# A vision tower on one core: group 0's patch embedding moved whole ahead of the class token's projections, the class chain on DVE behind the first normalisation

## The chip, the cores and the metric

The kernel runs on one core of one Trainium2 chip. The metric is the device time of one execution in microseconds (us). The engines are TensorE (PE, with its weight loads, PEld), VectorE (DVE), ScalarE (ACT), GpSimd (POOL) and SyncE (SP), which issues most of the transfers. Each engine runs its own instructions in order, and they wait for one another through semaphores.

## The reference

```python
patches = X.reshape(64, 3, 8, 28, 8, 28).transpose(0, 2, 4, 1, 3, 5).reshape(64, 64, 2352)
tokens = einsum('bpi,hi->bph', patches, W) + b              # 2352 -> 128
h = concatenate([class_token, tokens], axis=1) * pos_embed  # 65 rows per image
x = layernorm(h)
q, k, v = relu(x @ Wq.T + bq), relu(x @ Wk.T + bk), x @ Wv.T + bv   # 8 heads of 16
attn = softmax(einsum('bhnd,bhmd->bhnm', q, k) / (k.sum(-1, keepdims=True) + 1e-6))
h = h + (attn @ v) @ Wo.T + bo
# then layernorm twice, a shared swiglu network, and 2 of 8 experts by gates:
h = h + ffn(layernorm(h))
```

All is float32. The class token's row is the same in every image until attention has been done, so its normalised row, its q, k and v are computed once.

## The kernel before

The 64 images are worked in 8 groups of 8 images, 512 patch tokens each. The patch embedding of a group is a sum of 18 steps of 128 inputs (`NMAIN` = 18) and a tail of 48, in one PSUM bank `acc`; a step is two passes of PE in the profile. `patch(g, j0, j1)` issues the steps j0 to j1-1, and step 18 is the tail. The weights `w_patch` and the pixels `x_main` come in six pieces of three steps each (`PIECES`), each with its own semaphore. ACT's queue issues the loads of pieces 0 and 1 of the weights, then `const`, pieces 2 and 3, then the loads for the class token (`row_loads`: `rows`, `w_attn`, `bq_row`), and last pieces 4 and 5. SP's queue issues the pixels of group 0, then of group 1 as soon as the steps of group 0 have used a piece, then the weights of the feed-forward network.

Each engine has a prologue and then a `body(g)` for each group. `body(0)` is written out apart, so conditions on `last` (false for g = 0 alone) select what only group 0 has.

PE's prologue before (L638 to L657): 12 patch steps of group 0; wait for the class loads (`w_row`) and for the class row `hn_cls`; its transpose; 2 patch steps; wait for ACT's copy `hn_cls_t`; the class token's four small projections (q, k, v, and the bias bv through Wo) into bank `O`; 3 steps; transposes of `k_cls` and `qn_cls` into `C0`; the last step and the tail; `to_natural(0)` (transposes of `h_t` into `C1`); `AHEAD` = 6 steps of group 1; `normed_t(0)` (transposes of the normalised tokens `hn_nat`). Ahead of the bodies PE waits for `cdve` 19, that is for DVE's `k_sel`, which `k_sums` uses.

PE's body starts with `k_proj`, `q_proj`, `k_sums`, `v_proj`, `q_transpose`, then `score(g, 0)` to `score(g, 3)` with the steps of the next group between them (`fill`).

ACT's prologue before (L898 to L910): copy of `hn_cls_t`; copies of the two columns `k_cls_t` and `qn_cls_t`; four small copies of the class key into `k_bd`; `natural(0)` (`h_nat`); `normed_t(0)` (`hn_t`). Its body starts with a table load, `k_plain` (`k_t`), `k_blocks` (four copies into `k_bd`), `v_blocks` (two into `v_bd`), `q_masked` (two into `q_mask`). All ACT copies are recorded at the line of the helper `go`, L796.

DVE's prologue before (L1244 to L1297): the class row (`h_cls`, its moments, `hn_cls`); the class chain of 19 small operations that starts with `q_cls_raw` from bank `O` (wait for `cpe` 2) and ends with `k_sel` (L1292, which waits for `cact` 3, the two column copies of ACT) and `cc_col`; then `tokens(0)` (L1028, `h_t`), `norm1(0)` and `norm1_scale(0)` (`hn_nat`). Its body starts with `q_add` and `q_norm`, then the row maxima of the scores. POOL waits for `cdve` 16 ahead of its bodies, since `bias_residual` reads `bo2`.

Of the kernel before, what the change touches and what calls it, by code (L numbers as in the profile page):

```python
# [32 lines left out]
NPATCH = GRID * GRID  # L33
SEQ = NPATCH + 1
D = 128
IN_D = CHANNELS * PATCH * PATCH
NMAIN = IN_D // 128
# [13 lines left out]
AHEAD = 6  # L51
# [44 lines left out]
def vit_tower(nc, A, out):  # L96
    ctx = ExitStack()
    with ctx:
# [235 lines left out]
        def is_int(g, value):  # L334
            return isinstance(g, int) and g == value
# [55 lines left out]
        def _(pe):  # L391
# [7 lines left out]
            def patch(g, j0, j1):  # L399

                if j0 == 0:
                    need(pe, hT_done, g - 1)
                for j in range(j0, j1):
                    for i, (a, _) in enumerate(PIECES):
                        if j == a:
                            need(pe, x_in[i], g)
                            if isinstance(g, int) and g == 0:
                                pe.wait_ge(w_piece[i].sem, 16)
                    if j < NMAIN:
                        last = mm(acc[:, :], w_patch[:, j, :], x_main[:, j, :], start=(j == 0), stop=False)  # L410
                        if any(j == b - 1 for _, b in PIECES):
                            last.then_inc(x_used.sem, 1)
                    else:
                        need(pe, x_in[-1], g)
                        mm(acc[:, :], w_patch_tail[:, :], x_tail[:, :], start=False, stop=True)\  # L415
                            .then_inc(acc_full.sem, 1)
# [186 lines left out]
                last.then_inc(e_full.sem, 1)  # L603


            def class_scores():
                need(pe, cscore_done, GROUPS - 1)
                need(pe, hT_done, GROUPS - 1)
                for half in range(2):
                    last = nc.tensor.transpose(acc[:, half * 128:(half + 1) * 128],  # L610
                                               cls_scores[:, half * 128:(half + 1) * 128], ident)
                last.then_inc(tpe.sem, 1)
# [20 lines left out]
            def class_out():  # L633
# [1 line left out]
                mm(acc[0:IMAGES, 128:256], tc_attn_t[:, :], wo[:, :], start=True, stop=True).then_inc(tpe.sem, 1)  # L635


            patch(0, 0, 12)  # L638
            pe.wait_ge(w_first.sem, FIRST)
            pe.wait_ge(w_row.sem, ROW)  # L640
            pe.wait_ge(hcls_step.sem, 4)
            nc.tensor.transpose(B1[:, 0:128], hn_cls[:, :], ident).then_inc(cpe.sem, 1)
            patch(0, 12, 14)
            pe.wait_ge(cact.sem, 1)
            mm(O[:, 0:128], hn_cls_t[:, :], wq[:, :], start=True, stop=True)
            mm(O[:, 128:256], hn_cls_t[:, :], wk[:, :], start=True, stop=True)
            mm(O[:, 256:384], hn_cls_t[:, :], wv[:, :], start=True, stop=True)
            mm(O[:, 384:512], bv_col[:, 0:1].to_broadcast([128, 128]), wo[:, :], start=True, stop=True)\
                .then_inc(cpe.sem, 1)
            patch(0, 14, 17)  # L650
            pe.wait_ge(cdve.sem, 9)
            nc.tensor.transpose(C0[:, 0:128], k_cls[:, :], ident)
            nc.tensor.transpose(C0[:, 128:256], qn_cls[:, :], ident).then_inc(cpe.sem, 1)
            patch(0, 17, NMAIN + 1)
            to_natural(0)
            patch(1, 0, AHEAD)
            normed_t(0)  # L657

            def body(g, par):
                nxt, last = has_next(g), has_last(g)  # L660

                ahead = 0 if last else AHEAD

                def fill(j0, j1):
                    if nxt and j1 > ahead:
                        patch(g + 1, max(j0, ahead), j1)

                k_proj(g)
                if last and not is_int(g, 1):
                    gates(g - 1, TILES, 128)  # L670
                q_proj(g)
                if is_int(g, 1):
                    z_transpose(0)
                k_sums(g)
                v_proj(g)
                if is_int(g, 1):
                    gates(0, TILES, 128)
                    pe.wait_ge(wlo_done.sem, 4)
                if last:
                    ffn_in(g - 1, 0, TOK)  # L680
                    ffn_in(g - 1, 1, TOK)
                if not nxt:
                    class_scores()
                q_transpose(g)
                if last:
                    ffn_in(g - 1, 2, TOK)
                    ffn_in(g - 1, 3, TOK)
                fill(0, 1)
                score(g, 0)
                fill(1, 3)  # L690
                score(g, 1)
                fill(3, 5)
                prob_transpose(g, 0)
                fill(5, 6)
                prob_v(g, 0)
                score(g, 2)
                fill(6, 9)
                prob_transpose(g, 1)
                fill(9, 10)
                if not nxt:  # L700
                    expert(g - 1, 0, 128)
                prob_v(g, 1)
                if not nxt:
                    class_probs()
                score(g, 3)
                fill(10, 13)
                if not nxt:
                    counts(g - 1, TILES, 128)
                prob_transpose(g, 2)
                if nxt and last:  # L710
                    counts(g - 1, TILES, 128)
                fill(13, 14)
                if not nxt:
                    shared_out(g - 1, 0, 128, False)
                    shared_out(g - 1, 1, 128, False)
                    shared_out(g - 1, 2, 128, False)
                prob_v(g, 2)
                fill(14, 18)
                prob_transpose(g, 3)
                fill(18, NMAIN + 1)  # L720
                if nxt and last:
                    shared_out(g - 1, 0, 128, False)
                    shared_out(g - 1, 1, 128, False)
                elif not nxt:
                    shared_out(g - 1, 3, 128, True)
                    expert(g - 1, 1, 128)
                prob_v(g, 3)
                if nxt:
                    to_natural(g + 1)
                if nxt and last:  # L730
                    shared_out(g - 1, 2, 128, False)
                    shared_out(g - 1, 3, 128, True)
                    expert(g - 1, 0, 128)
                elif not nxt:
                    expert(g - 1, 2, 128)
                attn_transpose(g)
                if nxt and last:
                    expert(g - 1, 1, 128)
                out_proj(g)
                if nxt and last:  # L740
                    expert(g - 1, 2, 128)
                if nxt:
                    normed_t(g + 1)
                else:
                    class_values()
                if last:
                    expert(g - 1, 3, 128)
                if last:
                    expert(g - 1, 4, 128)
                if not nxt:  # L750
                    class_out()
                if nxt and last:
                    expert(g - 1, 5, 128)
                if last:
                    z_transpose(g)
                if not nxt:
                    expert(g - 1, 5, 128)
                if last:
                    expert(g - 1, 6, 128)
                    expert(g - 1, 7, 128)  # L760

            pe.wait_ge(cdve.sem, 19)
            groups(pe, body)

            L = GROUPS - 1
# [28 lines left out]
        def _(act):  # L794
# [102 lines left out]
                        act.dma_start(dst, src).then_inc(w_row.sem, 16)  # L897
            act.wait_ge(cpe.sem, 1)  # L898
            go(hn_cls_t[:, :], B1[:, 0:128]).then_inc(cact.sem, 1)
            act.wait_ge(cpe.sem, 3)  # L900
            go(k_cls_t[:, :], C0[:, 0:1]).then_inc(cact.sem, 1)
            go(qn_cls_t[:, :], C0[:, 128:129]).then_inc(cact.sem, 1)
            act.wait_ge(pool_init.sem, POOL_INIT)
            act.wait_ge(cact.sem, 3)
            for hp in range(HP):
                r = slice(32 * hp, 32 * hp + 32)
                go(k_bd[r, :, hp, NPATCH:SEQ], k_cls_t[r, 0:1].unsqueeze(2).to_broadcast([32, GROUP_IMAGES, 1]))\
                    .then_inc(cact.sem, 1)
            natural(0, 0)
            normed_t(0)  # L910

            def body(g, par):
                nxt, last = has_next(g), has_last(g)
                load_table(g, 0, ACT.Silu if last else ACT.Relu)
                k_plain(g)
                k_blocks(g)
                if is_int(g, 1):
                    z_out(0, TOK)
                v_blocks(g)
# [72 lines left out]
        def _(dve):  # L992
# [244 lines left out]
            def output(g, tiles, rows):  # L1237
# [16 lines left out]
            dve.wait_ge(hcls_step.sem, 3)  # L1254
            v.tensor_scalar(hn_cls[:, :], h_cls[:, :], cls_mv[:, 0:1], cls_rstd[:, 0:1], ALU.subtract, ALU.mult)\
                .then_inc(hcls_step.sem, 1)
            dve.wait_ge(cpe.sem, 2)
            v.tensor_tensor(q_cls_raw[:, :], O[:, 0:128], bq_row[:, :], ALU.add).then_inc(cdve.sem, 1)
            v.tensor_tensor(k_cls_raw[:, :], O[:, 128:256], bk_row[:, :], ALU.add).then_inc(cdve.sem, 1)
# [32 lines left out]
            v.tensor_scalar(k_sel[:, HEADS:16], const[:, C_HEAD:C_HEAD + HEADS], qn_cls_t[:, 0:1], None, ALU.mult)\  # L1292
                .then_inc(cdve.sem, 1)
            v.tensor_reduce(cc_col[:, :], cc_pick[:, :], AX.X, ALU.add).then_inc(cdve.sem, 1)
            tokens(0)
            norm1(0, 0)
            norm1_scale(0, 0)  # L1297


            def class_max():  # L1300
# [322 lines left out]
```

## Time and profile before

| | |
|---|---|
| median of three runs | 560.98 us (559.74 to 562.35) |
| span of the profiled execution | 562.2 us |
| PE busy | 502.9 us (89%) |
| DVE busy | 335.3 us (60%) |
| ACT busy | 179.7 us (32%) |
| POOL busy | 183.0 us (33%) |
| mean granted clock of PE | 0.923 |

The page gives no time of its own for the profiled execution beside its span, which is the time from the first to the last instruction. The busy shares are means over a start of about 100 us, in which the engines wait for one another, and a steady part up to about 460 us, in which PE is busy nearly all the time. The change is in the start, so its rows are read there.

### The profile page before, as it was taken

The page shows a single profiled execution, that of the slowest core. Times are in us where ns is not written, and L with a number is a line of the kernel's source. Part 1 is how long each engine was busy: PE and PEld are TensorE (multiplying, and loading weights), DVE is VectorE, ACT ScalarE, POOL GpSimd, SP SyncE. Part 2 cuts the span into 40 slices and gives each one's busy share as a digit, 9 for nine tenths or more (in the row PEclk, how much of TensorE's full clock was granted, in tenths as well). Part 3 has the DMA queues.
Part 4 walks back from the last instruction along what each step waited for, and adds up shares of the span by engine and source line. Part 5 has one row for each costly group of instructions (what it writes and reads, how often), then busy time and mean ns, then how long its engine had stood idle before and what let it go on. Part 6 is the DMA issues. An engine that isn't in the chain of part 4 may idle for free.

```text
span 562.2 us, 7098 instructions
## 1 busy us (share of the span) xinstructions
PE 502.9 (89%) x2241; PEld 353.4 (63%) x2241; DVE 335.3 (60%) x867; ACT 179.7 (32%) x334; POOL 183.0 (33%) x214
## 2 busy tenths in 40 slices
PE   5596885999999999999999999999999968698775
PEld 2244543855875587558755876587658756596563
DVE  0042358274776477647764777577756768935672
ACT  0015215342174216421642164216421652002320
POOL 6000006221271128112811182118211825226235
PEclk9788696599999999999999999999999998758988
DMA  8954150036004510451045104510000000000000
GB/s 342 366 179 175 45 187 1 0 112 211 22 0 131 193 41 1 132 179 53 0 131 174 57 0 129 172 61 1 20 1 0 2 19 1 0 1 1 18 2 21
DMA packets 14413, 44.71 MB, mean 80 GB/s; under 512 B 1721, under 2 KB 7090, under 8 KB 14386
## 3 DMA queue, kind: packets, MB, share of 16 engines
q1 hardware_dynamic: 12882, 42.39, 22.6%
q10 hardware_dynamic: 1504, 1.99, 1.1%
q8 instruction: 14, 0.23, 0.2%
q14 instruction: 13, 0.11, 0.1%
HBM read 42.24 MB, written 2.13 MB: 79 GB/s over the span
## 4 chain that ended last, share of the span: by engine, by line
PE 65%; DVE 17%; issue 7%; DMA 4%; POOL 4%; ACT 1%; ACTq 1%; DVEq 0%; POOLq 0%; SPq 0%
PE acc L410 21%; PE scores L471 6%; PE O L497 5%; PE B L396 4%; DMA bq_row<-in_bq_row 3%; DVE z_nat L1021 3%; PE acc L629 2%; DVE stats L1004 2%; PE B L453 2%; PE acc L415 2%; PE C L547 1%; POOL rstd L1446 1%; PE C L574 1%; DVE attn_nat L1113 1%; PE scores L549 1%
## 5 line engine op out<-in xcount | busy, mean ns | idle before, releaser
L410 PE MATMUL acc<-x_main,w_patch 128*128 128x512 f32 x288 | 141.4, 619 | 5.9 <-DMA w_patch<-in_w_patch 5.9
L410 PEld LDWEIGHTS acc<-x_main,w_patch 128*128 128x128 f32 x288 | 54.7, 200 | 50.3 <-issue 42.0
L1509 POOL TENSOR_TENSOR prod<-prod 128x512 f32<-128x512 f32 (+1 forms) x33 | 42.6, 1291 | 33.3 <-DVE prod L1233 33.3
L796 ACT ACTIVATE probs<-shift 128x512 f32<-128x512 f32 x32 | 20.4, 638 | 83.5 <-DVE shift L1073 83.5
L1502 POOL TENSOR_TENSOR hidden_lo<-silu,hidden_hi 128x512 fp32r<-128x512 f32 (+1 forms) x18 | 20.9, 1163 | 76.8 <-ACT hidden_hi L796 76.7
L497 PEld LDWEIGHTS O<-v_bd,probs_t 128*128 128x128 f32 x256 | 32.4, 195 | 21.2 <-ACT probs_t L796 11.9
L471 PE MATMUL scores<-k_bd,q_mask 128*128 128x260 f32 x128 | 38.9, 430 | 6.3 <-DVE shift L1073 3.1
L1069 DVE TENSOR_REDUCE row_max<-scores 128x8 f32<-128x520 f32 x32 | 22.3, 698 | 30.7 <-PE scores L471 30.3
L497 PE MATMUL O<-v_bd,probs_t 128*128 128x64 f32 (+1 forms) x256 | 35.4, 283 | 5.6 <-ACT probs_t L796 5.6
L1461 POOL TENSOR_TENSOR p_cls<-exp_cls,row_rec 128x16 f32<-128x16 f32 x16 | 5.4, 337 | 104.5 <-DVE row_rec L1088 100.0
L1442 POOL TENSOR_TENSOR rstd<-var,neg_half 128x4 f32<-128x4 f32 x8 | 8.1, 1015 | 87.0 <-DVE var L1017 87.0
L471 PEld LDWEIGHTS scores<-k_bd,q_mask 128*128 128x128 f32 x128 | 23.6, 205 | 19.0 <-DVE shift L1073 7.9
L796 ACT ACTIVATE probs_t<-B 128x512 f32<-128x512 f32 x32 | 19.0, 593 | 50.8 <-PE B L396 50.8
L1099 DVE TENSOR_TENSOR attn_patch<-O,row_rec 64x256 f32<-64x256 f32 x32 | 13.5, 422 | 32.4 <-PE O L497 31.9
L1021 DVE TENSOR_SCALAR z_nat<-h,mv,rstd 128x128 f32<-128x128 f32 (+1 forms) x33 | 28.8, 929 | 5.5 <-POOL rstd L1446 5.5
L1233 DVE TENSOR_TENSOR prod<-scores,comb 128x512 f32<-128x512 f32 (+1 forms) x33 | 22.6, 683 | 15.1 <-POOL routed L1516 9.8
L1233 DVE TENSOR_TENSOR prod<-C,comb 128x512 f32<-128x512 f32 (+1 forms) x33 | 22.0, 680 | 14.3 <-PE C L602 14.3
L600 PE MATMUL C<-w_eout_hi,hidden_hi 128*128 128x512 f32 (+1 forms) x66 | 29.2, 442 | 0.0
L600 PE MATMUL scores<-w_eout_hi,hidden_hi 128*128 128x512 f32 (+1 forms) x66 | 28.7, 435 | 0.0
L601 PE MATMUL C<-w_eout_lo,hidden_hi 128*128 128x512 f32 (+1 forms) x66 | 27.4, 415 | 0.0
L602 PE MATMUL C<-w_eout_hi,hidden_lo 128*128 128x512 f32 (+1 forms) x66 | 27.3, 413 | 0.0
L1511 POOL TENSOR_TENSOR prod<-prod 128x256 f32<-128x256 f32 (+1 forms) x33 | 26.2, 794 | 2.6
(239 smaller groups left out, 1052.6 us busy)
## 6 DMA issues: line engine op xcount, KB each, us to landing
x_main<-in_x_main SPq DMA_DIRECT2D x48, 768.0 KB, 4.2
out_tokens<-y_out SPq DMA_DIRECT2D x16, 128.0 KB, 2.5
w_patch<-in_w_patch ACTq DMA_DIRECT2D x6, 192.0 KB, 12.0
prod<-in_w_eout SPq DMA_DIRECT2D x2, 512.0 KB
x_tail<-in_x_tail SPq DMA_DIRECT2D x8, 96.0 KB, 3.1
silu<-in_w_in SPq DMA_DIRECT2D x2, 256.0 KB
hidden<-in_rows ACTq DMA_DIRECT2D x1, 256.0 KB, 14.9
w_attn<-in_w_attn ACTq DMA_DIRECT2D x1, 256.0 KB, 16.9
```

The costliest lines, as they stand in the source:

```text
L396: last = nc.tensor.transpose(dst[0:rows, t * 128:(t + 1) * 128], src, ident)
L410: last = mm(acc[:, :], w_patch[:, j, :], x_main[:, j, :], start=(j == 0), stop=False)
L471: last = mm(scores[:, b2, 0:HP * SEQ], q_mask[:, b, :, :].rearrange("p e n -> p (e n)"), k_bd[:, b, :, :].rearrange("p h m -> p (h m)"), s ...
L497: last = mm(O[:, c:c + 64], probs_t[p % 2][:, hp * 128:(hp + 1) * 128], pair, start=True, stop=True)
L600: mm(dst[0:rows, :], h_hi, w_hi, start=(c == 0), stop=False)
L601: mm(dst[0:rows, :], h_hi, w_lo, start=False, stop=False)
L602: last = mm(dst[0:rows, :], h_lo, w_hi, start=False, stop=(c == HC - 1))
L796: return nc.scalar.activation(dst, src, func, **kw)
L1021: v.tensor_scalar(dst[0:rows, t * 128:(t + 1) * 128], src[0:rows, t * 128:(t + 1) * 128], mv[0:rows, 0, t:t + 1], rstd[0:rows, t:t + 1], A ...
L1233: v.tensor_tensor(prod[t % 2][0:rows, half, :].rearrange("p (e d) -> p e d", d=D), src[0:rows, :].rearrange("p (e d) -> p e d", d=D), bcas ...
L1509: q.tensor_tensor(p[r, 0, :], p[r, 0, :], p[r, 1, :], ALU.add).then_inc(tree1_done.sem, 1)
L1511: q.tensor_tensor(p[r, 0, 0:2 * D], p[r, 0, 0:2 * D], p[r, 0, 2 * D:4 * D], ALU.add)\
```

## The change

Three orders are altered; no computation is added or taken away.

On PE all 18 steps of group 0 and the tail come first, the wait for the loads of the class token stands behind them, and then come the transpose of `hn_cls`, `to_natural(0)`, one step of group 1, the class token's projections, three steps, `normed_t(0)`, and two steps. The transposes of `k_cls` and `qn_cls` and the wait for `k_sel` move into the body of group 0, between `q_proj` and `k_sums`.

On ACT the copies of the two columns and the four class copies into `k_bd` move into the body of group 0, between `k_blocks` and `v_blocks`.

On DVE `tokens(0)`, `norm1(0)` and `norm1_scale(0)` move ahead of the class chain.

```diff
+            def class_columns():
+                pe.wait_ge(cdve.sem, 9)
+                nc.tensor.transpose(C0[:, 0:128], k_cls[:, :], ident)
+                nc.tensor.transpose(C0[:, 128:256], qn_cls[:, :], ident).then_inc(cpe.sem, 1)
+                pe.wait_ge(cdve.sem, 19)
...
-            patch(0, 0, 12)
+            patch(0, 0, NMAIN)
             pe.wait_ge(w_first.sem, FIRST)
+            patch(0, NMAIN, NMAIN + 1)
             pe.wait_ge(w_row.sem, ROW)
             pe.wait_ge(hcls_step.sem, 4)
             nc.tensor.transpose(B1[:, 0:128], hn_cls[:, :], ident).then_inc(cpe.sem, 1)
-            patch(0, 12, 14)
+            to_natural(0)
+            patch(1, 0, 1)
             pe.wait_ge(cact.sem, 1)
...
-            patch(0, 14, 17)
-            pe.wait_ge(cdve.sem, 9)
-            nc.tensor.transpose(C0[:, 0:128], k_cls[:, :], ident)
-            nc.tensor.transpose(C0[:, 128:256], qn_cls[:, :], ident).then_inc(cpe.sem, 1)
-            patch(0, 17, NMAIN + 1)
-            to_natural(0)
-            patch(1, 0, AHEAD)
+            patch(1, 1, 4)
             normed_t(0)
+            patch(1, 4, AHEAD)
...
                 q_proj(g)
+                if not last:
+                    class_columns()
...
-            pe.wait_ge(cdve.sem, 19)
             groups(pe, body)
...
-            act.wait_ge(cpe.sem, 3)
-            go(k_cls_t[:, :], C0[:, 0:1]).then_inc(cact.sem, 1)
-            go(qn_cls_t[:, :], C0[:, 128:129]).then_inc(cact.sem, 1)
-            act.wait_ge(pool_init.sem, POOL_INIT)
-            act.wait_ge(cact.sem, 3)
-            for hp in range(HP):
...
             natural(0, 0)
             normed_t(0)
+
+            def class_columns():
+                act.wait_ge(cpe.sem, 3)
+                go(k_cls_t[:, :], C0[:, 0:1]).then_inc(cact.sem, 1)
+                go(qn_cls_t[:, :], C0[:, 128:129]).then_inc(cact.sem, 1)
+                act.wait_ge(cact.sem, 3)
+                for hp in range(HP):
...
                 k_plain(g)
+                if not last:
+                    act.wait_ge(pool_init.sem, POOL_INIT)
                 k_blocks(g)
+                if not last:
+                    class_columns()
...
+            tokens(0)
+            norm1(0, 0)
+            norm1_scale(0, 0)
             dve.wait_ge(cpe.sem, 2)
             v.tensor_tensor(q_cls_raw[:, :], O[:, 0:128], bq_row[:, :], ALU.add).then_inc(cdve.sem, 1)
...
             v.tensor_reduce(cc_col[:, :], cc_pick[:, :], AX.X, ALU.add).then_inc(cdve.sem, 1)
-            tokens(0)
-            norm1(0, 0)
-            norm1_scale(0, 0)
```

## Rows read from the trace of the kernel before

**Rows 1.** Page, the chain that ended last, shares by engine.

```profile
PE 65%; DVE 17%; issue 7%; DMA 4%; POOL 4%; ACT 1%; ACTq 1%; DVEq 0%; POOLq 0%; SPq 0%
```

**Rows 2.** Timeline of PE: start, duration (us), engine, line, out<-in, count, idle before.

```profile
26.00 0.45 PE L642 MATMUL B<-const,hidden 128*128 128x128 f32 x1 [6.53 <-DVE hidden L1255]
26.24 3.63 PE L410 MATMUL acc<-x_main,w_patch 128*128 128x512 f32 x4
29.67 0.63 PE L645 MATMUL O<-w_attn,hidden 128*128 128x128 f32 x2
...
31.37 3.06 PE L410 MATMUL acc<-x_main,w_patch 128*128 128x512 f32 x6
...
37.90 5.32 PE L410 MATMUL acc<-x_main,w_patch 128*128 128x512 f32 x12
43.05 0.60 PE L396 MATMUL B<-const,hn_nat 128*128 128x128 f32 x4
44.43 1.10 PE L434 MATMUL B<-hn_t,w_attn 128*128 128x512 f32 x2 [0.78 <-ACT hn_t L796]
...
46.31 1.06 PE L447 MATMUL O<-k_sel,k_t 128*128 128x16 f32 x8
47.22 1.14 PE L453 MATMUL B<-w_attn,hn_t 128*128 128x128 f32 x8
...
51.52 1.18 PE L471 MATMUL scores<-k_bd,q_mask 128*128 128x260 f32 x4 [1.80 <-ACT q_mask L796]
54.22 2.10 PE L471 MATMUL scores<-k_bd,q_mask 128*128 128x260 f32 x4 [1.52 <-DVE shift L1073]
```

**Rows 3.** Timeline of ACT over 34 to 52 us, columns as in rows 2.

```profile
34.76 0.17 ACT L796 ACTIVATE qn_cls_t<-C 128x1 f32<-128x1 f32 x1
...
38.10 0.60 ACT L796 ACTIVATE h_nat<-C 128x512 f32<-128x512 f32 x1 [2.15 <-PE C L396]
...
45.57 0.69 ACT L796 ACTIVATE k_t<-B,const 128x512 f32<-128x512 f32 x1 [1.05 <-PE B L434]
46.15 2.79 ACT L796 ACTIVATE k_bd<-B,const 32x512 f32<-32x512 f32 x4
48.97 1.21 ACT L796 ACTIVATE v_bd<-B 64x512 f32<-64x512 f32 x2
50.20 1.26 ACT L796 ACTIVATE q_mask<-B,const 128x512 f32<-128x512 f32 x2
```

**Rows 4.** Issue of w_patch piece 4 (timeline), then its us to landing (transfers).

```profile
5.54 0.46 ACTq L891 DMA_DIRECT2D w_patch<-in_w_patch  x1
...
w_patch<-in_w_patch ACTq DMA_DIRECT2D x1, 192.0 KB, 20.3
```

**Rows 5.** Stretches: length, busy time of PE, PEld, DVE, ACT, POOL, clock, DMA.

```profile
26.00:32.00 6.00, 6.00 (x14) 3.63 (x15) 0.38 (x2) 0.28 (x1) 0.00 (x0) 0.50 0.20 81
...
50.00:52.00 2.00, 0.48 (x2) 0.46 (x3) 0.00 (x0) 1.53 (x4) 0.00 (x0) 1.00 0.08 30
52.00:54.00 2.00, 0.70 (x4) 0.22 (x2) 1.23 (x2) 0.00 (x0) 0.00 (x0) 0.62 0.00 0
```

**Rows 6.** Timeline of DVE over 31 to 49 us, columns as in rows 2.

```profile
31.62 0.29 DVE L1258 TENSOR_TENSOR hidden<-O,bq_row 128x128 f32<-128x128 f32 x1 [5.77 <-PE O L648]
...
35.72 0.23 DVE L1292 TENSOR_SCALAR k_sel<-const,qn_cls_t 128x8 f32<-128x8 f32 x1
...
36.60 0.75 DVE L1028 SCALAR_TENSOR_TENSOR h_t<-acc,const 128x512 f32<-128x512 f32 x1 [0.59 <-PE acc L415]
...
41.69 1.11 DVE L1021 TENSOR_SCALAR hn_nat<-h_nat,mv,rstd 128x128 f32<-128x128 f32 x4 [1.14 <-POOL rstd L1442]
...
48.02 0.69 DVE L1060 SCALAR_TENSOR_TENSOR q_nat<-q_nat,q_rec 128x512 f32<-128x512 f32 x1
```

**Rows 7.** Timeline of PE in the second group, columns as in rows 2.

```profile
99.25 1.73 PE L447 MATMUL O<-k_sel,k_t 128*128 128x16 f32 x8
100.82 2.06 PE L453 MATMUL B<-w_attn,hn_t 128*128 128x128 f32 x8
```

More of the change, by code:

```diff
@@ L899, in _ @@
             go(hn_cls_t[:, :], B1[:, 0:128]).then_inc(cact.sem, 1)
-            act.wait_ge(cpe.sem, 3)
-            go(k_cls_t[:, :], C0[:, 0:1]).then_inc(cact.sem, 1)
-            go(qn_cls_t[:, :], C0[:, 128:129]).then_inc(cact.sem, 1)
-            act.wait_ge(pool_init.sem, POOL_INIT)
-            act.wait_ge(cact.sem, 3)
-            for hp in range(HP):
-                r = slice(32 * hp, 32 * hp + 32)
-                go(k_bd[r, :, hp, NPATCH:SEQ], k_cls_t[r, 0:1].unsqueeze(2).to_broadcast([32, GROUP_IMAGES, 1]))\
-                    .then_inc(cact.sem, 1)
             natural(0, 0)
             normed_t(0)
+            def class_columns():
[4 more added lines that the diff above has]
+                for hp in range(HP):
+                    r = slice(32 * hp, 32 * hp + 32)
+                    go(k_bd[r, :, hp, NPATCH:SEQ], k_cls_t[r, 0:1].unsqueeze(2).to_broadcast([32, GROUP_IMAGES, 1]))\
+                        .then_inc(cact.sem, 1)
             def body(g, par):
```

## Prediction

> **What bounds the kernel now.** I read the page's chain first, then each engine's order of work over the first 60 us, then the granted clock there. The chain is mostly TensorE's (PE) [rows 1], but that is the average of a long steady part and a start of another kind, and every edit is in the start. The reader is to see three things there. First, PE stands still for 6.53 us until 26.00, when the class token's normalised row comes from DVE [rows 2]. Second, from 37 to 44 us the path is h_t on DVE, h_nat on ACT, the normalisation on DVE, a transpose on PE, hn_t on ACT, k_proj on PE. Third, from 45.57 us on ACT is the path: k_t, four k_bd copies, two v_bd, two q_mask, without a hole, and the first scores start at 51.52, right behind the last q_mask [rows 2, 3]. So whatever is put on ACT ahead of v_bd, or makes v_bd wait, is paid in full. From there to the second group softmax steps of DVE, ACT and PE follow one another; nothing in them can take back a late start of the scores.
>
> **What the early patches gain.** Before, PE runs after 26.00 one transpose, two patch steps (four passes), eight small class passes, three steps, two transposes, a step and the tail. Now all steps come first. They need w_patch piece 4, issued at 5.54 and landed 20.3 us later, at 25.84 [rows 4]. The weights thus come 0.16 us before the row for which PE waited: the 6.5 us hole can't be filled by this reordering, only its last 0.15 us. What is gained is the class work that leaves the path to the tail. At the low clock eight class passes take 31.37 - 29.67 = 1.70 us in the rows shown (29.67 is the first of four such pairs, each 0.43 later), and a patch pass (29.67 - 26.24) / 4 = 0.86; at the full clock a pass is 0.43 (12 in 5.32) [rows 2]. The clock is low from 26 to 32 us and full behind [rows 2, 5]; with PE as busy from 25.84 on I let it rise at the same moment, so what is taken out shortens the part at the full clock: 0.85 + 0.1 + 0.2 for the three transposes = 1.15, and 0.15 for the start: 1.3 to 1.4. If the low clock lasted through the tail it would be 2.3, so 1.2 to 2.3; I take 1.4, as the clock rose after six busy microseconds and nothing here changes that. The tail, and tokens(0) right behind it, comes at 35.2 instead of 36.60 [rows 6]. DVE is free then, as its class chain now stands behind.
>
> **The normalisation and k_proj.** h_nat goes from 38.10 to 36.7, and hn_nat, before done at 41.69 + 1.11 = 42.8, is done at 41.4 [rows 3, 6]. PE has from 36.0: four transposes 0.45, one patch step 0.86, the eight class passes 0.85, three steps 2.6, so it is ready at 40.8 and waits for DVE; before it was late, as its twelve patch passes ran to 43.05 [rows 2]. The transposes start at 41.5. But then two patch steps, 4 x 0.43 = 1.7 us, stand ahead of k_proj, where before PE waited only 0.78 us for hn_t. k_proj starts at 41.95 + 1.7 = 43.65 instead of 44.43: of a gain of 1.6 us, 0.8 is left. The two steps would have been run before in any case; nothing later gets shorter by them.
>
> **What the class chain costs.** k_sel, which k_sums reads, is written by DVE from qn_cls_t, and qn_cls_t is a copy on ACT that the change puts behind k_plain and all four k_bd copies. Step by step: k_proj 43.65, k_t 1.14 later at 44.8, the first k_bd 0.58 behind it at 45.4, the four take 2.79, to 48.2 [rows 2, 3]; two copies of a column, 0.24 (0.17 for the second, and 0.07 between their starts), to 48.4; k_sel on DVE 0.23, to 48.7 [rows 3, 6]. The rest isn't late: DVE's chain up to k_sel is 35.72 - 31.62 = 4.1 us, 41.4 to 45.5 [rows 6], and PE's two transposes wait only for a part of it and stand behind q_proj, at 45.4. So k_sums starts at 48.7 where it did at 46.31: 2.4 us late. Queued behind that one wait on PE are v_proj and everything else; behind k_sel on DVE are q_add and q_norm. q_add (0.69) ends at 49.6, k_sums has issued by 49.6 (47.22 - 46.31 = 0.9), v_proj ends 1.14 later at 50.8. ACT has meanwhile done its four small class copies (under 1 us, hidden), and waits. v_bd starts at 50.8, not 48.97: 1.8 late; 0.6 of the 2.4 is absorbed since v_bd queued behind k_bd before [rows 2, 3]. q_norm ends 2.4 behind the start of k_sums (48.02 + 0.69 - 46.31), at 51.1, and the transposes of q by 51.8, still under v_bd, to 52.0. q_mask follows at 52.0 for 50.20, and the scores at 53.35 for 51.52: **1.8 us late**, all on rows at the full clock. On POOL the wait for cdve 16 ends near 45 us; its next operation, the bias on h_nat, is wanted only by the residual some 40 us later. SP's transfers of the next groups and the ffn weights are issued a little earlier and are awaited later: nothing.
>
> **The clock.** Before, PE is busy 0.48 of 2.00 us in 50 to 52, and the clock falls within 52 to 54 [rows 5], in the last part of the first scores: these took 1.18 us, the next ones, at the low clock, 2.10 [rows 2]. A start 1.8 us later puts the first scores behind the fall: 0.9 more. And the change makes a hole on PE from 45.6 to 48.7, 3.1 us with nothing in it, so the fall may come already near 49: in the second group, at the low clock, the time from k_sums to v_proj is 100.82 - 99.25 = 1.57 (0.91 at the full) and v_proj takes 2.06 (1.14) [rows 2, 7], which moves v_bd by up to 1.4 more. Together 0 to 2.3 us. I take 0.9 and half of the 1.4, that is 1.6, as the scores' fall is nearly sure and the earlier one depends on how the hole lies. The Trainium skill (TensorE: Matmul & The Clock Gate, Terms) has a rule for the price: the penalty is the throttled time times one minus the granted share. By that rule low clock from 49.1 to 56.8 instead of from 52.5 to 52.7 would cost some 3.7 us; the rows give at most 2.3 since PE waits for ACT and DVE in part of that time.
>
> **Sum.** -1.4 (tail earlier) - 0.2 (normalised row not held by patches) + 0.8 (two steps ahead of k_proj) = -0.8 at k_proj; +3.2 on the way to k_sums (48.7 - 43.65 for 46.31 - 44.43) = +2.4; -0.6 = +1.8 at v_bd; +1.6 of clock = **+3.4 us**. The page gives a span of 562.2 us for the profiled execution, not its own time; the three runs lie from 559.74 to 562.35 with a median of 560.98, so the span is already 1.2 above the median. From 562.2 the span would be 565.6; from the median the forecast is 560.98 + 3.4 = 564.4.
>
> **Rivals.**
> (A) Forecast, wait for k_sel with some low clock: +2.3 to +4.8, 563.3 to 565.8. Chance 0.55.
> (B) The same wait, but the clock costs nothing net, as in the median run of before it fell ahead of the first scores too: +1.2 to +2.2, about 562.8. For it: the fall came only a microsecond into the scores. Chance 0.20.
> (C) The low clock is released a step later in the patch steps that fill PE between the later scores: say another eight passes at 0.86 instead of 0.43, which would be 3.4, of which some 1.9 not covered by waits for DVE, on top of +3.4: about 566.3. Chance 0.12.
> (D) The other side: the gain reaches the scores. That needs qn_cls_t to be on time, which is decided by when ACT gets to the two copies: only if it reaches them before 46 us does k_sums keep its place, and then v_bd gains the 0.8 of k_proj, up to 1.4 with the rest: 559.6 to 560.2. Against it speaks the code's order on ACT with 2.79 us of k_bd in front [rows 3]. Chance 0.06.
> (E) The edit does nothing measurable, since a late group 0 is taken up by waits before the steady part: 561. I see no such wait that isn't itself moved. Chance 0.07.
>
> **How the numbers follow.** Predicted is A, 564.4. The range leaves out D, most of E and the upper half of C: 561.5 to 567.0. About 0.5% (2.8 us) is what a measurement of this kernel can tell from no change: above 563.8 lie four fifths of A and all of C, 0.56; below 558.2 nothing that I worked out reaches, 0.04 for what I overlook; 0.40 between.
>
> **What would show it.** In the profile after: patch passes from 25.8 without a break to about 34.2; tokens(0) near 35.2; hn_nat done near 41.4; k_proj near 43.6; the copies to k_cls_t and qn_cls_t behind four k_bd copies, near 48.2; a hole on PE of 3 us ended by DVE's k_sel, k_sums near 48.7; v_bd near 50.8 or up to 1.4 later; the first scores after 53, at the low clock; and the steady part starting 2 to 5 us later. The prediction is wrong if k_sums starts before 47, if ACT's copies come ahead of k_bd, or if the second group starts no later than before.

## The result

The changed kernel has a median of 565.91 us (14 runs, 563.27 to 568.96), the kernel before 564.68 us (14 runs, 558.91 to 565.97, among them the three of the table of before). Runs of one kernel differ by much more than the kernels do; the ratio of the two is 1.0064 with a 95% interval of 1.0034 to 1.0094, about 3.6 us more, though the medians are only 1.2 apart. A second set of 12 runs gave 1.0028 (0.9989 to 1.0066). Over all sets, with the runs whose clock is listed, the changed kernel has a mean of 565.7 us (25 runs) and the kernel before 563.3 us (81 runs, 558.66 to 567.52): +2.4 us, 0.43%, with 1.5 to 3.4 as a 95% interval estimated from the spread. One more run of the changed kernel, of 570.57 us, counts as slow and is left out of the means, but it is the one whose profile is the second below. The kernel before had means of 563.1 to 563.5 in its three sets, so means are compared across sets.

The span of the changed kernel's profiled execution is 566.4 us, and the execution took 568.15 us: an execution is 1.8 us longer than its span. So the profiled execution of before, with its 562.2, took about 564.0 us, in the middle of its kind and not at its upper end.

Timeline of PE, changed kernel (columns as in rows 2):

```profile
25.80 7.34 PE L410 MATMUL acc<-x_main,w_patch 128*128 128x512 f32 x12 [6.49 <-DMA w_patch<-in_w_patch]
...
40.48 0.66 PE L396 MATMUL B<-const,hn_nat 128*128 128x128 f32 x4 [0.46 <-DVE hn_nat L1030]
40.97 1.88 PE L410 MATMUL acc<-x_main,w_patch 128*128 128x512 f32 x4
42.69 1.02 PE L434 MATMUL B<-hn_t,w_attn 128*128 128x512 f32 x2
...
47.78 1.07 PE L447 MATMUL O<-k_sel,k_t 128*128 128x16 f32 x8 [2.96 <-DVE cc_col L1306]
48.69 1.14 PE L453 MATMUL B<-w_attn,hn_t 128*128 128x128 f32 x8
50.24 1.12 PE L396 MATMUL B<-const,q_nat 128*128 128x128 f32 x4 [0.41 <-DVE q_nat L1069]
52.71 2.10 PE L471 MATMUL scores<-k_bd,q_mask 128*128 128x260 f32 x4 [1.36 <-ACT q_mask L800]
```

Timeline of ACT, changed kernel:

```profile
44.34 2.79 ACT L800 ACTIVATE k_bd<-B,const 32x512 f32<-32x512 f32 x4
...
47.22 0.17 ACT L800 ACTIVATE qn_cls_t<-C 128x1 f32<-128x1 f32 x1
...
49.87 1.21 ACT L800 ACTIVATE v_bd<-B 64x512 f32<-64x512 f32 x2 [1.52 <-PE B L453]
51.40 1.26 ACT L800 ACTIVATE q_mask<-B,const 128x512 f32<-128x512 f32 x2 [0.32 <-PE B L396]
```

Timeline of DVE, changed kernel:

```profile
34.23 0.75 DVE L1037 SCALAR_TENSOR_TENSOR h_t<-acc,const 128x512 f32<-128x512 f32 x1 [8.53 <-PE acc L415]
...
44.23 1.01 DVE L1301 TENSOR_TENSOR cc_pick<-cc_row,const 128x8 f32<-128x8 f32 x1
47.49 0.23 DVE L1304 TENSOR_SCALAR k_sel<-const,qn_cls_t 128x8 f32<-128x8 f32 x1 [2.25 <-ACT qn_cls_t L800]
```

The reader is to see the same chain as in rows 2, 3 and 6 with one link changed. The patches start when piece 4 has landed; h_t comes 2.4 us earlier than in rows 6 and k_proj 1.7 us earlier; then PE stands for 2.96 us behind DVE's k_sel, which stood 2.25 us for qn_cls_t, which stood behind k_bd. (The view names cc_col, the instruction behind k_sel; the wait in the code is for `cdve` 19, which is k_sel.) k_sums is 5.1 us behind k_proj (before 1.9), v_bd 7.2 (before 4.5), the first scores 10.0 (before 7.1). They start at 52.71 for 51.52, and at the low clock.

That is +1.2 us at the first scores. These run at the low clock, 2.10 us for 1.18, so the second scores start 2.1 us late (56.34 for 54.22). A part is then given back: in the six patch passes behind the third scores the clock rises earlier in the work than before,

```profile
64.82 3.96 PE L410 MATMUL acc<-x_main,w_patch 128*128 128x512 f32 x6
```

against, in the kernel before,

```profile
62.71 4.45 PE L410 MATMUL acc<-x_main,w_patch 128*128 128x512 f32 x6
```

k_proj of the second group starts 1.6 us late (90.97 for 89.34), that of the third 1.4 (160.68 for 159.27), that of the seventh 1.3 (387.20 for 385.87). So 1.4 of the 4.2 us in the span come from the start. The other 2.8 aren't in the start at all: k_proj of the eighth and last group is 5.9 us late (448.13 for 442.27), of which 1.7 come back by the end. Stretches of the changed kernel and of the kernel before (columns as in rows 5), at the same place of the work:

```profile
421.40:426.40 5.00, 5.00 (x25) 3.31 (x23) 0.75 (x1) 0.60 (x1) 0.00 (x0) 0.93 0.00 0
426.40:431.40 5.00, 5.00 (x21) 4.28 (x20) 3.65 (x17) 0.60 (x1) 0.00 (x0) 0.50 0.00 0
431.40:436.40 5.00, 5.00 (x16) 3.93 (x15) 2.55 (x7) 0.60 (x1) 1.01 (x1) 0.55 0.00 0
```

```profile
420.00:425.00 5.00, 5.00 (x28) 3.26 (x27) 0.75 (x1) 0.60 (x1) 0.00 (x0) 1.00 0.00 0
425.00:430.00 5.00, 5.00 (x32) 4.11 (x32) 4.30 (x18) 0.90 (x2) 0.55 (x1) 1.00 0.00 0
430.00:435.00 5.00, 5.00 (x29) 4.27 (x28) 4.46 (x19) 0.90 (x2) 0.72 (x2) 1.00 0.00 0
```

PE is busy throughout both, but in the changed kernel's execution the clock fell to half for 10 us near 426, in the last but one group, and in the execution of before it didn't. This is called the late fall below; it was in no step of the prediction.

### The profile page after: what moved, and what is told of

It reads as the page before. It is cut to its first block, busy times and chain, and to the rows that moved or that the text cites. A ratio compares the mean times of both kernels' runs of the same rounds, so it can differ in the third digit from the quotient of the medians.

```text
span 566.4 us, 7099 instructions
## 1 busy us (share of the span) xinstructions
PE 505.2 (89%) x2241; PEld 355.5 (63%) x2241; DVE 337.0 (60%) x867; ACT 179.7 (32%) x334; POOL 183.1 (32%) x214
## 4 chain that ended last, share of the span: by engine, by line
PE 65%; DVE 17%; issue 7%; DMA 4%; POOL 4%; ACT 1%; ACTq 1%; POOLq 0%; DVEq 0%; SPq 0%
PE acc L410 20%; PE scores L471 6%; PE O L497 5%; PE B L396 4%; DMA w_patch<-in_w_patch 4%; DVE z_nat L1030 3%; PE acc L635 2%; PE C L574 2%; DVE stats L1013 2%; PE B L453 2%; PE acc L415 1%; PE C L547 1%; POOL rstd L1455 1%; PE C L600 1%; PE scores L547 1%
## 5 line engine op out<-in xcount | busy, mean ns | idle before, releaser
L410 PE MATMUL acc<-x_main,w_patch 128*128 128x512 f32 x288 | 139.8, 613 | 13.3 <-DMA w_patch<-in_w_patch 13.3
L497 PEld LDWEIGHTS O<-v_bd,probs_t 128*128 128x128 f32 x256 | 33.8, 203 | 19.6 <-ACT probs_t L800 10.3
L497 PE MATMUL O<-v_bd,probs_t 128*128 128x64 f32 (+1 forms) x256 | 37.0, 291 | 3.9 <-ACT probs_t L800 3.9
L1037 DVE SCALAR_TENSOR_TENSOR h_t<-acc,const 128x512 f32<-128x512 f32 x8 | 6.0, 751 | 39.8 <-PE acc L415 39.8
```

Source lines behind the costliest of these rows:

```text
L497: last = mm(O[:, c:c + 64], probs_t[p % 2][:, hp * 128:(hp + 1) * 128], pair, start=True, stop=True)
```

## Experiments

**The changed kernel and the kernel before once more, with profiles.**

> The changed kernel once more, profiled and timed beside the kernel before on one chip. Theory 1 (the wait of k_sums for k_sel, late since ACT copies qn_cls_t only behind the four k_bd copies): k_sums starts 5.1 us after k_proj (before: 1.9) and v_bd 7.2 us after k_proj (before 4.5) in every execution, wherever the clock falls; time 2 to 4.5 us over the kernel before. Rival (the loss is only where TensorE's clock falls and rises, and the wait is harmless): the distances from k_proj stay, but in an execution with the same clock as before the first scores are no later than before, and the times of the two kernels overlap with no clear difference (under 1 us).

> The kernel before once more, for a second profile of it. Theory (part of the difference between executions of one kernel is where the clock falls): with the same order of instructions the start differs by under 2 us from the first profile, and a difference of the span beyond that lies in a stretch at the low clock that the other profile doesn't have. Rival: the difference lies in waits for transfers.

Measured for the changed kernel: 566.02 us median (560.15 to 570.57), ratio 1.0028 (0.9989 to 1.0066). The kernel before had 563.27 (559.2 to 567.23). The profiled execution is the one of 570.57 us, with a span of 568.8. Its clock rose at about 32, as in the first profile of before. Timeline of PE:

```profile
42.34 1.88 PE L410 MATMUL acc<-x_main,w_patch 128*128 128x512 f32 x4
44.06 1.02 PE L434 MATMUL B<-hn_t,w_attn 128*128 128x512 f32 x2
...
49.14 1.83 PE L447 MATMUL O<-k_sel,k_t 128*128 128x16 f32 x8 [2.95 <-DVE cc_col L1306]
50.81 2.06 PE L453 MATMUL B<-w_attn,hn_t 128*128 128x128 f32 x8
52.66 1.06 PE L396 MATMUL B<-const,q_nat 128*128 128x128 f32 x4
55.45 2.10 PE L471 MATMUL scores<-k_bd,q_mask 128*128 128x260 f32 x4 [1.73 <-ACT q_mask L800]
```

The 5.1 us from k_proj to k_sums stay. Here the clock fell already behind the hole: k_sums took 1.83 instead of 1.07 and v_proj 2.06 instead of 1.14, and the scores start at 55.45, 11.4 us behind k_proj and 3.9 later than in rows 2. The two profiles of one kernel differ by 2.7 us at this point: 1.4 ahead of k_proj, nearly all from when the clock rose (the patches also started 0.3 later), and 1.4 from when it fell behind the hole. That fall isn't peculiar to this execution: the one profiled below in the new order with the weights first (567.15 us), which has the same hole, has k_sums at 1.59 and v_proj at 2.05 us.

The kernel before took 565.38 us in its second profile, with a span of 563.6. Its start is within half a microsecond of the first (k_proj at 44.00 for 44.43), but the clock fell ahead of the first scores:

```profile
51.08 2.10 PE L471 MATMUL scores<-k_bd,q_mask 128*128 128x260 f32 x4 [1.80 <-ACT q_mask L796]
```

So first scores at the low clock aren't peculiar to the change. Nor did they cost anything in the end here, since the clock also rose sooner, within 60 to 62 us (0.79 there): k_proj of the third group is at 157.86, 1.4 us earlier than in the first profile. The late stretches of this execution:

```profile
418.00:423.00 5.00, 5.00 (x23) 2.86 (x22) 0.75 (x1) 0.60 (x1) 0.00 (x0) 1.00 0.00 0
423.00:428.00 5.00, 5.00 (x22) 4.39 (x21) 3.11 (x13) 0.60 (x1) 0.00 (x0) 0.50 0.00 0
428.00:433.00 5.00, 5.00 (x15) 3.92 (x15) 3.09 (x11) 0.39 (x1) 1.01 (x1) 0.50 0.00 0
```

So the late fall comes in the kernel before too, in some executions: it isn't made by the change. It cost 2.8 us here as well: third k_proj 1.4 earlier than in the first profile, span 1.4 longer. Whether the change makes it more frequent stays open: both profiles of the changed kernel have it and one of two of the kernel before.

**The two column copies first.** On ACT:

```diff
+                    class_columns()
                 k_blocks(g)
                 if not last:
-                    class_columns()
+                    class_keys()
```

`class_columns` is here the two copies alone, `class_keys` the class key's four.

> The changed kernel, but ACT copies the two class columns ahead of the four k_bd copies instead of behind them (the class key's own four copies stay behind). Theory 1: k_sums starts 2.6 to 2.9 us after k_proj instead of 5.1, the hole of 3 us on TensorE shrinks to under 1 us, v_bd starts about 6.1 us after k_proj instead of 7.2, the first scores 8.6 instead of 10.0, and the kernel is 1.4 to 3 us faster than the changed kernel, so within 1.5 us of the kernel before. Rival (two patch steps ahead of k_proj, or the clock by itself, cost the time): the time stays at that of the changed kernel within 0.5 us.

Measured: 562.55 us median (561.31 to 563.84), ratio to before 0.9985 (0.9953 to 1.0018). Rows of PE, then of ACT:

```profile
45.66 1.06 PE L447 MATMUL O<-k_sel,k_t 128*128 128x16 f32 x8 [0.74 <-DVE cc_col L1309]
...
51.45 2.10 PE L471 MATMUL scores<-k_bd,q_mask 128*128 128x260 f32 x4 [2.68 <-ACT q_mask L800]
```

```profile
45.09 0.17 ACT L800 ACTIVATE qn_cls_t<-C 128x1 f32<-128x1 f32 x1
45.14 2.79 ACT L800 ACTIVATE k_bd<-B,const 32x512 f32<-32x512 f32 x4
47.95 0.93 ACT L800 ACTIVATE k_bd<-k_cls_t 32x8 f32<-32x8 f32 x4
48.90 1.21 ACT L800 ACTIVATE v_bd<-B 64x512 f32<-64x512 f32 x2
```

k_proj was at 42.78, so k_sums came 2.9 us behind it, v_bd 6.1 and the scores 8.7: as expected. The whole loss against before is gone, 3.2 us in the means (562.6 for 565.7, expected 1.4 to 3), by moving two copies of 0.17 us. Now ACT is the path without a hole again. Not all of the 3.2 need be the wait: none of these 12 runs had more than 79.8 us of low clock (worked out below), and every profile with the late fall has over 92, so they probably went without it. By the same mark 8 of the 25 runs of the changed kernel had it and 23 of the 81 of the kernel before. The start alone gives 2.8: k_proj of the third group at 157.89 for 160.68.

**The hole filled with idle transposes.**

```diff
+                for _ in range(24):
+                    nc.tensor.transpose(scores[:, 0, 0:128], hn_nat[:, 0:128], ident)
                 pe.wait_ge(cdve.sem, 19)
```

> The changed kernel with 24 transposes whose result nobody reads (about 2.6 us at the full clock) put on TensorE in the hole between q_proj and k_sums; the wait for k_sel stays. Theory 1 with its clock term: k_sums keeps its place 5.1 us after k_proj, the low clock comes later than in the changed kernel, so that v_proj and the transposes of q run at the full clock in nearly all executions; 0.5 to 1.5 us faster than the changed kernel, still 1.5 to 3 us slower than the kernel before. Rival (the loss is all clock): the whole 2 to 4 us come back. Second rival (the clock in the hole costs nothing): no difference.

Measured: 562.94 us median (561.55 to 565.89), ratio to before 0.9994 (0.9961 to 1.0027). Timeline of PE:

```profile
45.19 2.78 PE L611 MATMUL scores<-const,hn_nat 128*128 128x128 f32 x24
48.32 1.06 PE L447 MATMUL O<-k_sel,k_t 128*128 128x16 f32 x8 [0.35 <-DVE cc_col L1308]
...
52.96 1.15 PE L471 MATMUL scores<-k_bd,q_mask 128*128 128x260 f32 x4 [1.52 <-ACT q_mask L802]
```

k_sums is still 5.1 us behind k_proj (43.22), but everything up to the first scores ran at the full clock, and 2.5 us come back in the means where 0.5 to 1.5 were expected. The first rival (all of it is clock) is nearer in size than my theory. It may not be the whole of it: the mean granted clock of these runs is 0.932 against 0.924 of before, and still they are no faster than before.

**The wait and the clock apart.** Each run lists its span and clock, so its time at the low clock, which is half of the full one, is span x (1 - clock) x 2. Over the 81 runs of before the time grows by 0.26 us for each us at the low clock (correlation 0.94), over the 25 of the changed kernel by 0.29. Read off the lines at 85 us of low clock, about the mean of before:

| kernel | mean, us | low clock, us | at 85 us of low clock |
|---|---|---|---|
| before | 563.3 | 85.1 | 563.3 |
| changed | 565.7 | 89.3 | 564.5 |
| copies first | 562.6 | 78.8 | 563.2 |
| hole filled | 563.2 | 76.0 | 565.0 |

The line for copies first is loose (12 runs, correlation 0.26), and both experiments' values at 85 lie outside most of their runs. For the changed kernel the difference of 2.4 us splits, as an estimate, into 1.2 at equal clock and 1.2 from 4.2 us more at the low clock. By this reading the hole filled keeps the first part (and a little more) and gives back the second with interest; the copies first give back both. The profiles have the start without the late fall. Start of k_proj by group, and the span:

| profile | first, us | third | seventh | eighth | span |
|---|---|---|---|---|---|
| before | 44.43 | 159.27 | 385.87 | 442.27 | 562.2 |
| before, second | 44.00 | 157.86 | 384.47 | 445.38 | 563.6 |
| changed | 42.69 | 160.68 | 387.20 | 448.13 | 566.4 |
| changed, second | 44.06 | 163.17 | 389.64 | 450.55 | 568.8 |
| copies first | 42.78 | 157.89 | 384.36 | 440.74 | 560.1 |
| hole filled | 43.22 | 158.60 | 385.22 | 441.60 | 560.9 |

At the third group the hole filled stands 2.1 us ahead of the changed kernel with the whole wait still in it, and between the two profiles of before. So in these profiles most of what the wait costs comes by way of the clock; that the wait costs 1.2 us by itself isn't shown.

**The first part alone.** Kernel before, with

```diff
-            patch(0, 0, 12)
+            patch(0, 0, NMAIN)
             pe.wait_ge(w_first.sem, FIRST)
+            patch(0, NMAIN, NMAIN + 1)
```

and without the three patch calls behind it.

> The kernel before with the first part alone: all patch steps of group 0 ahead of the class token's transpose and projections on TensorE; on DVE the class chain stays ahead of the first tokens, on ACT the class copies ahead of h_nat. Theory: the tail of the patch sum is done at 34 to 35 us (before: 36.6), but the class projections end only near 36.5, the class chain on DVE takes 4.4 us behind them, and h_t starts near 40.8 instead of 36.6: k_proj 4 us later, the kernel 3.5 to 5 us slower than before. Rival (the order of patch steps on TensorE is what sets the start): k_proj 1 to 2 us earlier than before.

Measured: 568.93 us median (566.88 to 572.04), ratio 1.0111 (1.0078 to 1.0145). PE, then DVE:

```profile
34.60 1.12 PE L415 MATMUL acc<-x_tail,w_patch_tail 48*128 48x512 f32 x2
...
51.20 1.10 PE L434 MATMUL B<-hn_t,w_attn 128*128 128x512 f32 x2 [0.78 <-ACT hn_t L794]
```

```profile
41.85 0.74 DVE L1026 SCALAR_TENSOR_TENSOR h_t<-acc,const 128x512 f32<-128x512 f32 x1
```

The sum is done early and lies for 6 us, until DVE has done the class chain; k_proj came 6.8 us late and the mean is 5.9 us over before (4, and 3.5 to 5, expected: the wait for the chain also let the clock fall, and `to_natural` and some patch steps ran at half rate). The move on DVE is what makes the move on PE worth anything.

**The weights ahead of the class loads, in both orders.**

```diff
-                elif i == 3:
+                elif i == len(PIECES) - 1:
                     for dst, src in row_loads:
```

> The changed kernel, with ACT's queue issuing w_patch pieces 4 and 5 ahead of the three loads for the class token. Theory (the 6.5 us hole on TensorE after step 11 is the wait for piece 4, which queues behind those loads): pieces 4 and 5 land near 19 us, all patch steps of group 0 are done near 25.5 at the full clock, the class loads land near 28 instead of 23.5, so the class row comes at 30.4 and h_t, which stands behind it on DVE, near 31 instead of 34 to 35.5; k_proj near 39; 3 to 5 us faster than the changed kernel. Rival (the transfers share one rate and the hole only moves): h_t within 1 us of the changed kernel, no difference in time.

> The kernel before with the same edit of ACT's queue (w_patch pieces 4 and 5 ahead of the class loads). Theory: TensorE there waits for the class row between steps 11 and 12 whatever the weights do, and the class row now comes at 30.4 instead of 25.9, so the hole grows to 11 us, k_proj comes 4 to 5 us later and the kernel is 3 to 5 us slower than before. Rival (the weights set the hole in both orders): no slower than before.

Measured in the new order: 561.99 us median (559.92 to 567.26), ratio 0.999 (0.995 to 1.003); in the old order: 566.32 us (562.95 to 569.12), ratio 1.0063 (1.0027 to 1.0098). PE in the new order, then in the old:

```profile
6.07 18.65 PE L410 MATMUL acc<-x_main,w_patch 128*128 128x512 f32 x36 [6.07 <-DMA w_patch<-in_w_patch]
24.65 1.12 PE L415 MATMUL acc<-x_tail,w_patch_tail 48*128 48x512 f32 x2
30.84 0.45 PE L649 MATMUL B<-const,hidden 128*128 128x128 f32 x1 [5.07 <-DVE hidden L1264]
```

```profile
30.48 0.45 PE L642 MATMUL B<-const,hidden 128*128 128x128 f32 x1 [11.00 <-DVE hidden L1255]
```

All 18 steps and the tail ran on one another to 25.8, so the 6.5 us hole was the queue's doing. The old order, tied to the class row, loses by the same edit: its hole is 11.00 us and its mean 2.9 us over before, a little under the 3 to 5 expected. In the new order 5 us of hole stay, now behind the tail, since the class row stands ahead of h_t on DVE and ahead of `to_natural` on PE. h_t came at 30.61 and k_proj at 40.41, 3.7 earlier than in the second profile of the changed kernel. In the means 2.4 us were gained on the changed kernel, less than the 3 to 5 expected: the hole ahead of k_sums is unchanged, and in this profile the clock fell there and again near 425.

**Patch steps in the hole.** `AHEAD = 9`, and `patch(1, 6, AHEAD)` ahead of the wait for k_sel.

> The changed kernel with AHEAD 9 instead of 6: patch steps 6 to 8 of group 1 (2.6 us at the full clock) stand in the hole ahead of k_sums, and are gone from the softmax stage, where before they ran between the third scores and the next transposes at the low clock. Theory: k_sums stays 5.1 us after k_proj, the first scores as in the kernel with the hole filled by idle transposes, and the stage behind the third scores is shortened by the steps taken out, up to 3 us; 2 to 5 us faster than the changed kernel, so 0 to 2.5 us faster than before. Rival (TensorE waits for DVE and ACT there in place of the steps): no faster than the kernel with idle transposes, 562.9.

Measured: 561.33 us median (558.87 to 564.0), ratio to before 0.997 (0.9941 to 1.0). PE:

```profile
45.02 2.74 PE L410 MATMUL acc<-x_main,w_patch 128*128 128x512 f32 x6
48.14 1.06 PE L447 MATMUL O<-k_sel,k_t 128*128 128x16 f32 x8 [0.37 <-DVE cc_col L1307]
```

4.5 us less than the changed kernel and 1.9 less than with idle transposes, in the means: the hole's steps are gone from the stage behind the third scores, though not all of their 2.7 us came back. Against before the gain of 2.0 in the means is at the edge of what the runs can tell.

**Small passes spread, late.** In each group but the first and the last, two tiles of the shared network's output go between patch steps 14 to 17.

> The changed kernel; only PE's order late in each group's softmax stage is altered: the first two tiles of the shared network's output (small passes) go between the patch steps 14 to 17 instead of behind the tail. Nothing of the start changes. Theory (a part of the times is a fall of the clock near 425 us, in a stretch of small passes, which some executions have and others don't, and which costs 2 to 3 us): with the small passes spread the fall doesn't come, the low clock is under 2 us of the stretch 400 to 480 us, the times lie within 5 us of one another instead of 10, and the mean is 1 to 2.5 us below the changed kernel's. Rival (the spread of the times comes from the start alone): the times stay spread over 8 to 10 us.

Measured: 565.09 us median (561.02 to 567.59), mean 564.8. A stretch of its profile, then of the changed kernel's:

```profile
400.00:480.00 80.00, 72.41 (x353) 52.46 (x352) 57.15 (x143) 28.93 (x57) 29.87 (x30) 0.96 0.02 4
```

```profile
400.00:480.00 80.00, 74.26 (x329) 53.87 (x327) 53.46 (x136) 28.32 (x56) 26.18 (x30) 0.87 0.02 4
```

The low clock takes 0.04 x 80 x 2 = 6.4 us of this stretch, where under 2 was expected, and 20.8 in the changed kernel. The profiled execution, whose clock had taken the same course as the changed kernel's up to 112 us, didn't have the late fall, and its span was 563.3 for 566.4. But over the runs the times still spread over 6.6 us and the mean fell by only 0.9. The fall explains that pair of profiles; it doesn't explain the spread of all runs. That the edit prevented it isn't shown either: of the twelve profiles eight are without it, and seven of these don't have the edit. Since only profiled executions show where the clock fell, how often it comes stays open.

**A version that beats both.** The weights first as above; on DVE `tokens(0)` and `norm1(0)` ahead of the class row and `norm1_scale(0)` ahead of `hn_cls`; on POOL and ACT the matching order; on PE `to_natural(0)`, five steps and `normed_t(0)` ahead of the class row's transpose, the class projections behind k_proj, three patch steps in the hole.

> A version meant to beat both: w_patch pieces 4 and 5 ahead of the class loads; on DVE the tokens and the normalisation of group 0 ahead of the class row, whose moments are taken while POOL works; on TensorE to_natural(0), five steps of group 1 and normed_t(0) ahead of the class row's transpose, the class projections behind k_proj, and three more patch steps of group 1 in the hole ahead of k_sums. Theory: h_t near 25.8, k_proj near 33.4, k_sums near 39.5, first scores near 45 instead of 51.5, 7 to 11 us faster than before. Rival (the class chain, now last, takes the gain): k_sums near 44, under 3 us faster.

Measured: 555.59 us median (553.75 to 556.93), ratio to before 0.9881 (0.9838 to 0.9924). PE:

```profile
24.58 1.12 PE L415 MATMUL acc<-x_tail,w_patch_tail 48*128 48x512 f32 x2
...
33.61 1.02 PE L434 MATMUL B<-hn_t,w_attn 128*128 128x512 f32 x2
...
40.79 1.06 PE L447 MATMUL O<-k_sel,k_t 128*128 128x16 f32 x8 [1.58 <-DVE k_sel L1308]
...
45.54 2.10 PE L471 MATMUL scores<-k_bd,q_mask 128*128 128x260 f32 x4 [1.35 <-ACT q_mask L804]
```

7.7 us less than before in the means. The first scores are 6 us earlier than in rows 2; k_sums came 1.3 later than expected, of which 0.8 is cc_pick, which took 1.01 us beside POOL, and the rest the later start of the chain.

## Why the prediction was right or wrong

**The hole at the start.** Right: the patches started at 25.80 for 25.84, bound by piece 4, and the experiment on the queue showed that cause.

**The tail earlier.** Forecast -1.4. With the clock rising at the same moment (the second profile of the changed kernel and the first of before), h_t came at 35.60 for 36.60; as the patches started 0.3 us later there than forecast (26.12 for 25.84), -1.3. In the first profile the clock rose within 29 to 30 us and not at 32 (granted clock 0.63 in that microsecond), so that h_t came at 34.23, a microsecond earlier than forecast. The forecast had let the clock rise at the same moment; where it rises differs between executions.

**k_proj.** Right in its parts: 42.69 - 40.48 = 2.2 us from the transposes to k_proj with the two steps between, forecast 2.15. By the clock's earlier rise k_proj as a whole came 1.7 us earlier than before and not 0.8; in the second profile it was 0.4.

**The wait for k_sel.** Right in place and size: 5.1 us to k_sums, forecast 5.05; 7.2 to v_bd, forecast 7.15. Removing its cause alone, with two copies moved, brought the time back to before. Only the transposes of q weren't hidden under v_bd: at the low clock they took 1.12 us for 0.63, and q_mask waited 0.32 for them.

**The clock: the step that failed.** The sum has +1.6 for it, 0.9 for the first scores at the low clock and half of 1.4 for a fall right behind the hole, and lets all of it last to the end, since "nothing in them can take back a late start of the scores". The events came: the scores ran at the low clock in both profiles of the changed kernel, and the early fall came in one, the execution of 570.57 us, where it moved v_bd by 8.84 - 7.18 = 1.66 us. But their price was another:

- The 0.9 is no cost of the change in every execution: in the second profile of the kernel before the first scores ran at the low clock too.
- The softmax stage did give back: the clock rose earlier in the work (six patch passes in 3.96 for 4.45 us). In the first profile v_bd, ahead of all that the 1.6 stands for, is late by -1.7 + 3.2 - 0.6 = +0.9 (49.87 for 48.97), and k_proj of the third group by 1.4. So 0.5 was left of the 1.6, and +1.4 of the +3.4. In the second profile it is 3.9 - 2.2 = 1.7, in a run far above the mean of its kernel. Over all runs the estimate is 1.2.
- It was counted only up to the scores. 2.8 of the 4.2 us between the first two profiles are the late fall, in the last but one group, of which no row was read for the prediction.
- The wait and the clock aren't two separate costs of 1.8 and 1.6. The experiment that only kept PE busy in the hole gave back 2.5 us, not 0.5 to 1.5, with the wait in place.

The rule of the Trainium skill (TensorE: Matmul & The Clock Gate, Terms) would set 4.2 us more at half rate at an estimated 2.1. The runs disagree: their slope is 0.26 to 0.29 per us and not 0.5. A likely reason is that PE waits for others in part of the low stretches (0.70 of 2.00 us busy from 52 to 54, rows 5).

**The size and the base.** Forecast +3.4 us (0.61%). The ratio of the first set is 0.64% with its interval from 0.34 to 0.94%, but the medians of that set give only +1.2, and the means over all sets +2.4 (0.43%, 1.5 to 3.4). The place and the length of the wait were right; the sum was at the upper edge or too large, by the clock term. That the ratio of the first set meets the forecast so closely is luck: the other measures of the same difference are lower. The base failed plainly too. Three runs with a median of 560.98 lie low in a kernel whose runs go from 558.66 to 567.52 and whose mean over 81 is 563.3; I took the span of 562.2 to be 1.2 above it where the execution, 1.8 longer than its span, was 3.0 above. So 564.4 was forecast from the wrong place: base and difference together would have been 563.3 + 2.4 = 565.7.

**The rivals.** D (the gain reaches the scores) is excluded for this order, but copies first shows what decides it, as it said: when ACT gets to the two copies. B and A can't be told apart by the time: 565.7 - 563.3 = 2.4 lies on their border. For B speak the second profile of before, which has what B rests on (the clock falls ahead of the first scores there too), and the +1.4 at the third group. E doesn't hold in the profiles: the third group still starts 1.4 us late. By the times the first set and all sets together exclude no change, the second set alone doesn't. C (the low clock released a step later in the patch steps) is refuted in both profiles: the six passes behind the third scores took 3.96 and 3.82 us for 4.45, so the release came earlier in the work, though later on the time axis.

## What to carry to other kernels

When a step that reads a small late value is moved, look at the in-order queue that makes the value: here two copies of 0.17 us behind 2.8 us of others set a wait of 3 us, and moving them cost nothing. What a hole on TensorE costs can lie mostly in the clock behind it: 24 idle transposes in it gave back 2.5 us, useful patch passes 4.5. A low stretch that starts earlier can end earlier too, so follow a loss to the same instruction of later groups before it is added to the sum. And where runs of one kernel spread over 8 us, three of them are no base: take many runs, and read where the clock falls in the whole trace, not only near the edit.

## What was unexpected

The clock fell to half near 425 us while PE was busy 5.00 of 5.00 us in the rows on both sides of the fall, in the second profile of before as in the changed kernel's. What ran there are many small passes (128 and 64 columns, and matmuls of 9 rows) instead of 512 columns; that these are the cause isn't shown. And cc_pick on DVE, 0.17 us for 8 columns before, took 1.01 us when POOL's bias_residual ran beside it, from 43.95 for 1.26 us in the changed kernel and likewise in the version that beats both. In the changed kernel this cost nothing, as k_sel waited longer for ACT; with the copies first and in the version that beats both it is on the path to k_sums.
